# Four first-layer tiles moved into the drain of the attention loop, and part of the low halves moved from POOL to DVE

## What is computed

```
scores = softmax(x @ wg + bg)                    # x: normed input, [32, 128, 256]
top-2 experts per token; masked = scores * mask
route  = masked / (masked.sum(0) + 1e-6) * 32
per expert and sequence: the 64 tokens with the highest route (max_len = S // 2)
h   = gelu(x @ w1[e] + b1[e])                    # 64 hidden columns for each of 16 experts
out = h @ w2[e] + b2[e]                          # added at the chosen tokens only
z   = x + outs;  layer norm(z) * gamma + beta;  added to the residual
```

## Time and profile before

| | |
|---|---|
| median of 3 runs | 570.81 us (569.54 to 571.08) |
| the profiled execution | 572.44 us, its span 570.7 us |
| mean granted clock of PE | 0.963 |
| PE matmuls busy | 526.0 us, 92% of the span, 6063 |
| DVE busy | 453.3 us, 79% |
| POOL busy | 387.5 us, 68% |
| ACT busy | 357.1 us, 63% |

### The profile page before, as it was taken

One profiled execution on the slowest core, in us unless ns is written; L12 is line 12 of the kernel. 1 busy time (PEld: TensorE's weight loads), 2 busy tenths in 40 slices (PEclk: granted clock), 3 DMA queues, 4 the chain that ended last, 5 costly groups with the idle time before them and its releaser, 6 DMA issues. The chain is left out here.

```text
span 570.7 us, 16170 instructions
## 1 busy us (share of the span) xinstructions
PE 526.0 (92%) x6063; PEld 395.0 (69%) x6063; DVE 453.3 (79%) x1019; ACT 357.1 (63%) x744; POOL 387.5 (68%) x512
## 2 busy tenths in 40 slices
PE   4797788999999999999999999839999999999985
PEld 2697666778777777777777777624457777777774
DVE  5785466889888888888888888977846888887776
ACT  1215767788787877878778787614584655565540
POOL 3050235888787877878778787942095977898783
PEclk9957799999999999999999999987999999999998
DMA  6800000000000000000000000000633044053011
GB/s 208 325 2 1 2 1 2 4 3 2 3 3 3 2 3 3 3 3 3 4 3 2 4 3 3 2 0 2 151 85 83 20 110 102 22 141 85 24 45 55
DMA packets 11905, 21.73 MB, mean 38 GB/s; under 512 B 4668, under 2 KB 9780, under 8 KB 10164
## 3 DMA queue, kind: packets, MB, share of 16 engines
q1 hardware_dynamic: 11828, 20.71, 13.1%
HBM read 16.24 MB, written 4.33 MB: 36 GB/s over the span
## 5 line engine op out<-in xcount | busy, mean ns | idle before, releaser
L768 POOL TENSOR_TENSOR s_pl<-s_pf,s_ph 128x512 f16<-128x512 f32 x128 | 147.0, 1160 | 15.3 <-ACT s_ph L860 15.3
L949 DVE TENSOR_REDUCE s_mx<-ps 128x4 f32<-128x512 f32 x128 | 83.8, 677 | 29.1 <-PE ps L1090 29.1
L1503 PE MATMUL ps<-s_xt_all,s_w1s 128*128 128x512 f16 x384 | 89.9, 387 | 0.8 <-PEq L751 0.8
L1526 PE MATMUL ps<-s_w2s,s_hid 128*128 128x256 f16 x768 | 88.9, 273 | 0.0
L854 ACT ACTIVATE s_pf<-ps 128x512 f32<-128x512 f32 x128 | 76.6, 602 | 16.9 <-PE ps L1103 16.9
L1526 PEld LDWEIGHTS ps<-s_w2s,s_hid 128*128 128x128 f16 x768 | 75.1, 98 | 11.1
L860 ACT ACTIVATE s_ph<-s_pf 128x512 f16<-128x512 f32 x128 | 77.2, 637 | 0.0
L1136 PE MATMUL ps<-s_zh,s_cth 128*128 128x256 f16 x256 | 69.8, 273 | 0.0
L1136 PE MATMUL ps<-s_zl,s_cth 128*128 128x256 f16 x256 | 69.8, 273 | 0.0
L1136 PE MATMUL ps<-s_zh,s_ctl 128*128 128x256 f16 x256 | 69.8, 273 | 0.0
L1503 PEld LDWEIGHTS ps<-s_xt_all,s_w1s 128*128 128x128 f16 x384 | 38.1, 100 | 42.4 <-issue 4.5
(11 more groups left out here) (230 smaller groups left out, 1252.3 us busy)
## 6 DMA issues: line engine op xcount, KB each, us to landing
s_rep<-picks SPq DMA_DIRECT2D x14, 512.0 KB, 6.6
s_stage<-in_w SPq DMA_DIRECT2D x2, 1024.0 KB, 13.9
out<-s_ot_a SPq DMA_DIRECT2D x16, 128.0 KB, 1.7
out<-s_lg SPq DMA_DIRECT2D x16, 128.0 KB, 1.7
s_stage<-in_wq SPq DMA_DIRECT2D x1, 1024.0 KB, 4.7
s_stage<-in_wk SPq DMA_DIRECT2D x1, 1024.0 KB, 6.4
s_stage<-in_wv SPq DMA_DIRECT2D x1, 1024.0 KB, 8.1
s_stage<-in_wo SPq DMA_DIRECT2D x1, 1024.0 KB, 9.9
```

The costliest lines, as they stand in the source:

```text
L768: nc.gpsimd.tensor_tensor(flat(pl[:, b % 2, 4 * j:4 * j + 4, :]), pf[:, j, :], flat(ph[:, b % 2, 4 * j:4 * j + 4, :]), ALU.subtract).then_ ...
L949: nc.vector.tensor_reduce(mx[:, b % 2, c:c + 4], A[ab][:].rearrange("p (h k) -> p h k", h=4), AX.X, ALU.max).then_inc(max_done[hf][ab], 1)
L1503: mm = nc.tensor.matmul(HB[j % NH][:], w1s[:, wp, c, j * P:(j + 1) * P], xt_all[:, GB * g:GB * (g + 1), xp, c, :], start=(k == 0), stop=(k ...
L1526: mm = nc.tensor.matmul(zb[b % 4], hid[:, g % 2, hp, j, t * P:(t + 1) * P], w2s[:, wp, j, :], start=False, stop=(j == NJ - 1 and hp == 1))
```

## The change

1. In the second block PE makes four tiles of group 0: (0, 0) in step 30 ahead of `x_cols(30)`, and (0, 1), (0, 2), (0, 3) in step 31 ahead of `x_cols(31)`. The four banks of `HB` are banks 0 to 3, which the loop used for queries and scores; the tiles wait for the last readers of these, which are behind them by then.
2. In the third block PE starts with tile 4. `routes` comes behind tile 9, that is behind six tiles of the block, where four stood.
3. On ACT the copies of `FIRST_MASKS` start ahead of the Gelu of (2, 5): `hi(0, 0)`, `gelu(2, 5)`, `hi(0, 1)`, `gelu(2, 6)`, `hi(0, 2)`, `gelu(2, 7)`, and the other seven copies.
4. The low parts of (0, 6) and (0, 7) are made by DVE, between its masks of group 0 and those of group 1; POOL makes the other low parts. Waits that counted POOL's low parts count accordingly, and `experts_out(0)` also waits for DVE's two.
5. `hidden_beside(0)` gives four tiles instead of two, and each later b starts two tiles further on, and the last tile comes two tiles' worth earlier (39 tiles are given by the end of b = 23 where 37 were).

```diff
+        def hidden_tile(g, j):
+            k = 0
+            for c in range(KC):
+                for wp, xp in ((0, 0), (0, 1), (1, 0)):
+                    mm = nc.tensor.matmul(HB[j % NH][:], w1s[:, wp, c, j * P:(j + 1) * P],
+                                          xt_all[:, GB * g:GB * (g + 1), xp, c, :], start=(k == 0), stop=(k == 5))
+                    k += 1
+            mm.then_inc(h_ready, 1)
...
+                def first_hidden(j):
+                    if j < 2:
+                        pe.wait_ge(max_done[1][j], B)
+                    else:
+                        pe.wait_ge(exp_done[j], B)
+                    pe.wait_ge(xlo_done, GB)
+                    hidden_tile(0, j)
...
+                    if i == B - 2:
+                        first_hidden(0)
+                    if i == B - 1:
+                        for j in (1, 2, 3):
+                            first_hidden(j)
                     if has(i):
                         x_cols(i)
...
-            first, last = (min((n * 40 + 25) // 26, NJ * (NG - LEAD)) for n in (b, b + 1))
+            first, last = (min((n * 40 + 25) // 26 + 2, NJ * (NG - LEAD)) if n else 0 for n in (b, b + 1))
...
+        def lo_by_dve(g, j):
+            return g == 0 and j >= 6
+
+        def lo_count(g, j):
+            return min(j + 1, 6) if g == 0 else NJ * g + j - 1
...
                 for g, j in FIRST_MASKS:
-                    lo(g, j)
+                    if not lo_by_dve(g, j):
+                        lo(g, j)
...
-                    if g >= 3:
-                        act.wait_ge(glo_done, NJ * (g - 3) + j + 1)
+                    if g >= 3 and lo_by_dve(g - 3, j):
+                        act.wait_ge(glo_front, j - 5)
+                    elif g >= 3:
+                        act.wait_ge(glo_done, lo_count(g - 3, j))
...
                 for j in range(NJ):
+                    if j >= 5:
+                        hi(*FIRST_MASKS[j - 5])
                     gelu(LEAD - 1, j)
-                    hi(*FIRST_MASKS[j])
-                for g, j in FIRST_MASKS[NJ:]:
+                for g, j in FIRST_MASKS[NJ - 5:]:
                     hi(g, j)
...
-                for g, j in FIRST_MASKS:
+                for g, j in FIRST_MASKS[:NJ]:
+                    masked(g, j)
+                for j in (6, 7):
+                    dve.wait_ge(ghi_done, j + 1)
+                    nc.vector.tensor_tensor(hid[:, 0, 1, j, :], gelu_tile(0, j), hid[:, 0, 0, j, :], ALU.subtract).then_inc(glo_front, 1)
+                for g, j in FIRST_MASKS[NJ:]:
                     masked(g, j)
...
                     if t == 0:
-                        pe.wait_ge(glo_done, NJ * (g + 1))
+                        pe.wait_ge(glo_done, lo_count(g, NJ - 1))
+                    if b == 0:
+                        pe.wait_ge(glo_front, 2)
...
-                for g in range(LEAD):
-                    for j in range(NJ):
-                        hidden(g, j)
-                        if (g, j) == (0, 3):
-                            routes()
+                for n in range(NH, NJ * LEAD):
+                    hidden(n // NJ, n % NJ)
+                    if n == 9:
+                        routes()
```

More of the change, by code:

```diff
@@ L749, in build @@
         STEPS = range(-6, B + 1)
+        NH = 4
+        HB = psum[0:NH]
+        h_ready = sem("h_ready")
+        def hidden_tile(g, j):
[6 more added lines that the diff above has]
+            mm.then_inc(h_ready, 1)
         with nc.Block() as block:
@@ L1221, in build @@
         PAIRS = 5
-        NH = 4
         b2_rows = (32, 64)
@@ L1233, in build @@
         vz, rz = sb("vz", [P, 4]), sb("rz", [P, 4])
-        HB, ZB, RTB = psum[0:NH], psum[4:8], psum[7]
+        ZB, RTB = psum[4:8], psum[7]
         gr_rows = both(gr).rearrange("p (g h j f) -> p g h f j", g=NG, h=2, j=NJ)
@@ L1274, in build @@
         out_st = [sem(f"out_st{n}") for n in range(4)]
-        h_ready, gelu_done, gm_done, ghi_done, glo_done, z_ready4 = (
-            sem(n) for n in ("h_ready", "gelu_done", "gm_done", "ghi_done", "glo_done", "z_ready4"))
+        gelu_done, gm_done, ghi_done, glo_done, glo_front, z_ready4 = (
+            sem(n) for n in ("gelu_done", "gm_done", "ghi_done", "glo_done", "glo_front", "z_ready4"))
         nmr_ok, xn_ok, zt_ok, bsz_ok, zstat, vz_ok, rz_ok, zs_ok, hb_ok, o_ok = (
@@ L1499, in hidden @@
                         pe.wait_ge(gelu_done, n - NH + 1)
[L1500 to L1506, removed]
+                    hidden_tile(g, j)
                 def routes():
```

## The result

The changed kernel takes 572.43 us (median of 20 runs, 570.16 to 574.01), the kernel before 570.76 (20 runs, 569.28 to 572.25). The ratio is 1.0027, with a 95% interval of 1.0017 to 1.0037: 1.5 us slower, with 1.0 to 2.1 us as the bounds of the interval. The forecast was 572.0.

A forecast was written before the change was run, and what follows sets the result against it. PE, without idle time from the first output to 535 us, was taken as the bound, so what moves that output moves the rest: 425.7 against 424.41, +1.3, less 0.1 for the tail, +1.2 on 570.81 gives 572.0 us; range 568.9 to 574.4.

The forecast's parts named there:

- T0: Start of the block behind the attention loop: 386.68 us in the profile before, forecast at 386.4.
- R: Start of the routes' transposes on PE, on which DVE's selection hangs: 394.49 us before, forecast 399.9, 5.4 us later.
- the pair of DVE and POOL: Before the first output: one DVE and one POOL operation side by side take about 1.605 us; six pairs, 9.6 us.
- rival 5: In the drain: tile 0 delays `x_cols(30)` and `output(31, 1)`, holding up the next block by up to 1.3 us; chance 0.05.
- The edit alone is worth nothing here: On ACT: starting copies ahead of later tiles gains nothing, since both the tiles and the masks have moved back.
- The first: Behind the drain: PE's clock holds, first output at 423.1, 1.3 us earlier, total 569.5 us; chance 0.13.
- the third: Full clock and less contention together: PE has its 24 tiles at 421.0, 3.4 us earlier, total 567.4 us; chance 0.05.
- The second: Before the first output: less DVE and POOL contention, clock low, PE sets it at 423.65, total 570.0 us; chance 0.10.
- The fourth: PE's 2.05 us gap before the first output drops the clock again, losing 1.7 us, total 573.7 to 574.6; chance 0.12.

The follow-up runs named there:

- the last two kernels: Four tiles and their Gelus in the drain, routes behind tile 8, first copy ahead of Gelu (2, 3): 567.03 us; the same plus eight unread matmuls in the drain: 565.97 us.
- the fastest kernel: Changed kernel with four tiles ahead of `x_cols(31)`, their Gelus in the drain, routes behind tile 8, first copy ahead of Gelu (2, 3): 567.03 us, ratio 0.9919.

## Why the prediction was right

**What held.** The forecast, 1.2 us slower, met 1.7 by the medians and 1.5 by the ratio. Its steps, from T0 or R (T0 itself from the transposes of `turn(31, 1)`, 372.64 before and 370.73 after):

| step | forecast | trace after |
|---|---|---|
| tile 0 | free | 1.65 us |
| tiles 1 to 3 in the drain | free | free (1.75 us of wait left) |
| `x_cols(31)` | 0.44 | 0.44 |
| T0 behind the transposes | 13.8 | 15.2 |
| tile 4 | T0 + 3.1 | T0 + 3.1 |
| clock when tile 4 starts | low | low, to 392.2 |
| `routes` | T0 + 13.5 | T0 + 12.5 |
| first mask | R + 13.6 | R + 13.5 |
| POOL's first low part | R + 16.2 | R + 16.2 |
| six low parts to the first output | 9.6 | 9.3 |
| first output | T0 + 39.3 | T0 + 38.0 |
| first output to the end | as before, less 0.1 | 146.4, before 146.3 |

The tail gave nothing back for its two tiles, the pair of DVE and POOL came at 1.6 us, and the chain shows the wait for the table load that the argument rested on. Three tiles in the drain instead of four, and the Gelus moved along with the tiles, show the wait from both sides, and the matmuls that nobody needs show that the low clock behind it costs time.

**What was off.** `routes` was 1.0 earlier, since the clock came back sooner after tile 4 in this trace. Tile 0 was taken at nothing, with 1.3 as its bound (rival 5, chance 0.05): it cost 1.65 in the trace after, and the same in two other traces of kernels that have it, while it was free in four. In this trace T0 is 1.4 later than forecast, and the first output is 1.3 earlier behind T0. That the sum meets the forecast to 0.1 us here is luck. In the three other traces that have the same order up to `routes` (low parts back on POOL, two tiles in front, ACT's order of before) the clock was full at tile 0, and there both steps came as forecast: T0 13.8 behind the transposes and `routes` at T0 + 13.4 to 13.5. So the working fits the executions that meet the full clock in the loop. The rival should have had a much larger chance, and its bound of 1.3 was too low. The error was to read the clock in the loop from one trace, where it was full. (The block that the prediction calls the second, behind the loop, is the third.)

**What the first output waits for.** In seven traces (the changed kernel, tile 0 in the second wait, three tiles, two in front, ACT's order of before, and the last two kernels) the first output comes 25.5 to 25.6 us behind R, for R from T0 + 7.4 to T0 + 13.5; the prediction had 25.8. From `routes` on it is the selection, the masks and the low parts on DVE and POOL that count; PE has its tiles earlier in all seven and stands idle for 0.3 to 4.2 us before the output. The sum followed POOL's low parts alone. In eight of the twelve experiments it is DVE's second low part that ends last, 0.1 us ahead of the first output. In the changed kernel it ends at 422.78, 1.0 ahead of POOL's last.

**Copies.** "The edit alone is worth nothing here" holds in the changed kernel (old order: no difference), but as worked out it hid that the edit puts the first copy four tiles later. The kernel without tiles in the drain showed it, against my expectation.

**Rivals.** The first (the clock holds) is out, and the third with it: the clock was low at tile 4 in every trace in which PE waited for the Gelu with nothing else to do. The second (less contention, PE sets the first output) is out: PE waited 1.59 us there, and the low parts took 1.6 us each. The fourth (a second low clock before the first output) did not come in the changed kernel, but did where the wait was 3.21, 4.15 or 4.7 us; the two tiles in front keep it off. Its 1.7 us was taken from a low stretch two thirds as long, for which the prediction had no row; in two of the three traces the first output took 1.7 us more.

**What stays open.** How often tile 0 meets the low clock over many runs: the edit that moves it gave 0.9 us by the ratios, but its interval reaches to the changed kernel. Why the matmuls that nobody needs gave 2.5 us where their trace shows 0.8. And whether filling the drain adds anything in the fastest kernel.

## What to carry to other kernels

Work moved ahead of a block fills its buffers there, and its worth ends where the next piece waits for the first reader of a buffer: follow that reader back (here an Exp and a table load) before counting the tiles. With the reader moved along (and tile 0 and the routes placed better) the move paid: 3.6 us faster instead of 1.5 slower; with the wait kept and filled it was 2.2 faster. Where a wait on PE is long enough for its clock to fall, taking useful work out of it can cost time though the wait would cover it (1.6 us here for two tiles). And when work is shared between two engines, see which of them ends last: a wait on both semaphores is met by the later one, and the profile may name the other.

## What the runs showed of the hardware

- DVE with two SBUF operands and POOL, 128x512 each: 0.69 and 1.15 us alone, 1.64 and 1.60 side by side. One of each goes by in 1.6 us, somewhat less than the 1.75 of one behind the other (0.615 and 1.13 from start to start). (The Trainium skill, "SBUF — State Buffer", SBUF: two separate sides, has the two take a shared port in turn, each for its whole instruction; by that a pair would be the full 1.75. The trace agrees in kind and is 0.15 lower, 1.6.)
- The same matmuls in the last steps of the loop ran at the full clock in some traces and at half in others, at 371 to 376 us, with a wait of 1.65 before them in both. The wait at the start of the loop is alike: a low clock followed in six of the fourteen traces, where the wait was 2.82 or 2.83 us, and not in the eight where it was 2.55 to 2.60. What makes the difference stays open.
- Waits of PE before the first output of 1.6 and 1.9 us left the clock full. With waits of 3.2, 4.15 and 4.7 us it fell to 1.2 GHz (1.0 us before the end of the first, 0.1 and 0.4 us behind the start of the output in the others) for 6.8, 3.4 and 3.4 us, and the first output took 5.3, 4.4 and 4.4 us instead of 2.74.
- An ACT table load takes 1.28 us each time, also for going back and forth; two more of them in the drain, where ACT was mostly idle, cost at most 0.2 us at the start of the next block.
